# Sending row maxima and reciprocals to all lanes over memory, from the second batch on

## The reference

```
q = (layernorm(x) @ Wq + bq)            # 4 batches x 256 rows, 32 heads of 128
k, v = split(ctx @ Wkv + bkv)           # 4 batches x 1601 context rows, 8 kv heads of 128
scores = einsum("blkgd,bmkd->bkglm", q, k) / sqrt(128)
attn = softmax(scores, axis=-1)
o = einsum("bkglm,bmkd->blkgd", attn, v)
x = x + tanh(g_xattn) * (o @ Wo + bo)
x = x + tanh(g_ffn) * ffn(layernorm(x)) # base matrix, top 2 of 8 LoRA experts
```

## Time and profile before

| | |
|---|---|
| time, median of 3 runs | 2336.55 us (2336.43 to 2344.85) |
| the profiled execution's own time | 2337.85 us |
| its span, first to last instruction | 2335.9 us |
| busy: PE, DVE, ACT, POOL | 98%, 78%, 72%, 70% |
| mean granted TensorE clock | 0.996 |

### The profile page before, as it was taken

The page is one execution under the profiler, slowest core; times in us unless marked ns, Lnnn a source line. Parts: engine busy times, 40 slices in busy tenths (PEclk is TensorE's granted clock), DMA queues, the critical chain, the costliest instruction groups (busy, mean ns, idle before and its releaser), DMA issues.

```text
span 2335.9 us, 37750 instructions
## 1 busy us (share of the span) xinstructions
PE 2289.8 (98%) x12569; PEld 1956.9 (84%) x12569; DVE 1822.1 (78%) x3162; ACT 1685.2 (72%) x3208; POOL 1631.9 (70%) x1372
## 2 busy tenths in 40 slices
PE   7999999999999999999999999999999999999988
PEld 6888888888888888888888888888888888888864
DVE  5887888879778787877878778787878768778775
ACT  4776777767777776777767777776777767777763
POOL 5897987967667786866757867774865757656672
PEclk9999999999999999999999999999999999999999
DMA  7444334354133233335133243223423122122211
GB/s 256 147 147 142 117 129 144 133 201 144 59 124 114 93 122 100 98 108 185 59 104 105 77 133 115 102 92 115 143 82 109 66 79 82 46 100 73 82 37 54
DMA packets 122591, 258.11 MB, mean 111 GB/s; under 512 B 13344, under 2 KB 46624, under 8 KB 122144
## 3 DMA queue, kind: packets, MB, share of 16 engines
q1 hardware_dynamic: 122400, 255.71, 32.4%
HBM read 188.81 MB, written 66.86 MB: 109 GB/s over the span
## 4 chain that ended last, share of the span: by engine, by line
PE 87%; DVE 5%; POOL 4%; ACT 2%; issue 2%; DMA 0%; ACTq 0%; SPq 0%; POOLq 0%; DVEq 0%
PE psW L381 13%; PE psW L382 12%; PE psW L383 12%; PE psW L577 7%; PE psS L383 7%; PE psS L381 7%; PE psS L382 7%; PE psW L579 7%; PE psW L578 7%; PE psW L436 2%; PE psW L444 2%; POOL xs L766 2%; POOL pl L770 1%; DVE mrun L1194 1%; DVE psum_ L1221 1%
## 5 line engine op out<-in xcount | busy, mean ns | idle before, releaser
L766 POOL TENSOR_TENSOR xs<-xs,mb 128x512 f32<-128x512 f32 (+1 forms) x832 | 1069.2, 1314 | 518.1 <-ACT mb L837 518.1
L1194 DVE TENSOR_TENSOR mrun<-psS,mrun 128x512 f32<-128x512 f32 (+1 forms) x704 | 483.9, 687 | 380.3 <-ACT xs L837 377.7
L837 ACT ACTIVATE xs<-psS 128x512 f32<-128x512 f32 (+1 forms) x832 | 496.7, 597 | 212.2 <-PE psS L383 202.6
L930 ACT ACTIVATE ph<-xs 128x512 fp32r<-128x512 f32 (+1 forms) x832 | 520.6, 626 | 0.9 <-PE psW L579 0.9
L991 DVE TENSOR_TENSOR pl<-psP,ph 128x512 fp32r<-128x512 f32 (+1 forms) x672 | 459.5, 684 | 54.8 <-ACT ph L930 49.0
L1221 DVE TENSOR_TENSOR psum_<-psP,psum_ 128x512 f32<-128x512 f32 (+1 forms) x672 | 457.3, 681 | 0.0
L927 ACT ACTIVATE psP<-xs 128x512 f32<-128x512 f32 (+1 forms) x672 | 402.4, 599 | 3.0 <-POOL xs L766 1.5
L381 PE MATMUL psS<-ql,kh 128*128 128x512 f32 (+1 forms) x832 | 344.1, 414 | 1.1 <-DVE ql L1014 1.1
L577 PE MATMUL psW<-ph,vh 128*128 128x512 f32 (+1 forms) x832 | 336.6, 405 | 5.8 <-POOL pl L770 4.0
L383 PE MATMUL psS<-qh,kl 128*128 128x512 f32 (+1 forms) x832 | 328.1, 394 | 0.0
L382 PE MATMUL psS<-qh,kh 128*128 128x512 f32 (+1 forms) x832 | 328.1, 394 | 0.0
(11 more groups left out here) (185 smaller groups left out, 4562.5 us busy)
## 6 DMA issues: line engine op xcount, KB each, us to landing
wqh<-scr_wq SPq DMA_DIRECT2D x96, 256.0 KB, 2.6
wql<-scr_wq SPq DMA_DIRECT2D x96, 256.0 KB, 2.9
woh<-scr_wo SPq DMA_DIRECT2D x48, 512.0 KB, 3.3
wol<-scr_wo SPq DMA_DIRECT2D x48, 512.0 KB, 4.4
scr_wq<-wqh SPq DMA_DIRECT2D x32, 256.0 KB, 2.0
scr_wq<-wql SPq DMA_DIRECT2D x32, 256.0 KB, 2.5
scr_wo<-woh SPq DMA_DIRECT2D x16, 512.0 KB, 2.6
scr_wo<-wol SPq DMA_DIRECT2D x16, 512.0 KB, 4.0
```

Source lines behind the costliest of these rows:

```text
L766: eng.tensor_tensor(tile, tile, mb[0:rows_of(t), U % 2, :], ALU.subtract).then_inc(s_sub)
L837: return eng.activation(hi, src, ACT.Copy)
L930: eng.activation(ph[0:rows, T % RP, :], xs[0:rows, T % RX, :], ACT.Exp).then_inc(s_h)
L1194: eng.tensor_tensor(run, psS[0:rows, s % 2, :], a, ALU.max).then_inc(s_m)
```

## The change

For units 16 to 61 the maxima, and for units 16 to 60 the reciprocals, no longer pass through PE and ACT. SP writes the 128 x 4 values to a small tensor in memory (2 KB), waits for that, and reads it back with a broadcast over partitions, 512 values on each of 128 lanes (256 KB), straight into `mb` or `rbc`. The jobs `b` and `r` go for these units, and the other jobs are laid out anew in `AT_MEM`. DVE makes `nm` and `rinv` first in its slot, ahead of the running maximum. The multiplication by `rbc`, `oh`, `ol` and `o0` come one slot later. So that the values lie in memory in the right order, the transposes of `m` and `s` take every fourth column.

```diff
+    MEM_LO, MEM_MAX, MEM_SUM = 16, UN - 2, UN - 3
+    def max_by_mem(U):
+        return MEM_LO <= U < MEM_MAX
+    def sum_by_mem(U):
+        return MEM_LO <= U < MEM_SUM
+    def by_pe(U, by_mem):
+        return sum(not by_mem(u) for u in range(U + 1))
+    def on_slot(V):
+        return 9 if sum_by_mem(V) else 8
 ...
+    AT_MEM = [
+        "m q0 k3 - q1 s v0 v1 v2 v3 - o0 o1",
+        "m,v4 v5 q0 v6 k0 s,v7 q1 k1 v8 v9 v10 o0 o1",
+        "m,v11 k2 v12 q0 k3 s - - q1 - - o0,x0 o1,x1",
+        "m q0 - k0 q1 s k1 - - k2 - o0 o1",
+    ]
-                    UN + 1: "- - - - - s - r - - o0 o1"}.get(U, AT[U % 4])
+                    UN + 1: "- - - - - s - r - - o0 o1"}.get(U, (AT_MEM if U >= 2 and sum_by_mem(U - 2) else AT)[U % 4])
+                if kind == "b" and max_by_mem(n) or kind == "r" and sum_by_mem(n):
+                    continue
 ...  TensorE
+                    cols = src.rearrange("l (p k) -> l k p", k=4)[:, k, :] if every_fourth else src[:, k * 128:(k + 1) * 128]
+                    m = eng.transpose(o[:, k * 128:(k + 1) * 128], cols, ident[:, :])
-                if s % NT == 10 and s // NT >= 2:
+                if s // NT >= 2 and s % NT == on_slot(s // NT - 2) + 2:
                     emptied(("pv", s // NT - 2, 0), s_ol, s // NT - 1)
 ...  SyncE
+            def max_to_lanes(n):
+                i = n - MEM_LO
+                sp.wait_ge(s_nm, n + 1)
+                if i >= 2:
+                    sp.wait_ge(s_md, 16 * (i - 1))
+                eng.dma_start(scr_m[n % 2], nm[:, n % 2, :]).then_inc(s_mw, 16)
+                sp.wait_ge(s_mw, 16 * (i + 1))
+                if n >= 2:
+                    sp.wait_ge(s_sub, NT * (n - 1))
+                eng.dma_start(mb[:, n % 2, :], scr_m[n % 2].rearrange("p k -> (p k)").partition_broadcast(128)).then_inc(s_md, 16)
+            def sum_to_lanes(n):
+                # the same with s_r, rinv, scr_r, s_rw, s_on, rbc and s_rd
 ...
             for s in range(SLOTS):
+                if t == 1 and max_by_mem(U - 1):
+                    max_to_lanes(U - 1)
+                if t == 6 and sum_by_mem(U - 2):
+                    sum_to_lanes(U - 2)
 ...  GpSimd, in take_off
+                if max_by_mem(U):
+                    pool.wait_ge(s_md, 16 * (U - MEM_LO + 1))
+                else:
+                    pool.wait_ge(s_mb, by_pe(U, max_by_mem))
 ...  ScalarE
-                if s % NT == 8 and 0 <= V < UN:
+                if 0 <= V < UN and s % NT == on_slot(V):
                     act.wait_ge(s_on, V + 1)
 ...  VectorE
+            def goes_first(kind, n, part):
+                return kind == "m" and max_by_mem(n) or kind == "s" and sum_by_mem(n)
             for s in range(SLOTS):
+                for j in jobs.get(s - 1, []):
+                    if goes_first(*j):
+                        after_job(*j)
 ...
-                if t == 8 and 0 <= U - 2 < UN:
+                if 0 <= V < UN and t == on_slot(V):
                     dve.wait_ge(s_pv, NT * (V + 1))
+                    if sum_by_mem(V):
+                        dve.wait_ge(s_rd, 16 * (V - MEM_LO + 1))
+                    else:
+                        dve.wait_ge(s_rb, by_pe(V, sum_by_mem))
```

More of the change, by code:

```diff
@@ L19, in gated_block @@
 def gated_block(nc: bass.Bass, x, ctxT, gx, gf, wq, bq, wk, wv, bkv, wo, bo, bw, rw, la, lb,
-                scr_x, scr_b, scr_w, scr_c, out):
+                scr_x, scr_b, scr_w, scr_c, scr_m, scr_r, out):
     F32 = mybir.dt.float32
@@ L221, in gated_block @@
         s_out = sem("s_out")
+        s_mw = sem("s_mw")
+        s_md = sem("s_md")
+        s_rw = sem("s_rw")
+        s_rd = sem("s_rd")
         s_s = sem("s_s")
@@ L431, in proj_q, with turn @@
                 emptied(("q", U, h), s_ql, 2 * U + h + 1)
-            def turn(key, src, done, by, v):
+            def turn(key, src, done, by, v, every_fourth=False):
                 o = take(key)
                 for k in range(4):
-                    m = eng.transpose(o[:, k * 128:(k + 1) * 128], src[:, k * 128:(k + 1) * 128], ident[:, :])
+                    cols = src.rearrange("l (p k) -> l k p", k=4)[:, k, :] if every_fourth else src[:, k * 128:(k + 1) * 128]
+                    m = eng.transpose(o[:, k * 128:(k + 1) * 128], cols, ident[:, :])
                 m.then_inc(done)
@@ L505, in job @@
                     pe.wait_ge(s_m, 12 * (n + 1))
-                    turn(("m", n, 0), mrun[:, n % 2, :], s_mt, s_nm, n + 1)
+                    turn(("m", n, 0), mrun[:, n % 2, :], s_mt, s_nm, n + 1, max_by_mem(n))
                 elif kind == "s":
@@ L513, in job @@
                         pe.wait_ge(s_ap, 2 * (n - NU + 1))
-                    turn(("s", n, 0), psum_[:, n % 2, :], s_su, s_r, n + 1)
+                    turn(("s", n, 0), psum_[:, n % 2, :], s_su, s_r, n + 1, sum_by_mem(n))
                 elif kind == "b":
                     pe.wait_ge(s_nm, n + 1)
-                    spread(("b", n, 0), nm[:, n % 2, :], s_bt, s_mb, n + 1)
+                    spread(("b", n, 0), nm[:, n % 2, :], s_bt, s_mb, by_pe(n, max_by_mem))
                 elif kind == "r":
                     pe.wait_ge(s_r, n + 1)
-                    spread(("r", n, 0), rinv[:, n % 2, :], s_rt, s_rb, n + 1)
+                    spread(("r", n, 0), rinv[:, n % 2, :], s_rt, s_rb, by_pe(n, sum_by_mem))
                 elif kind == "x":
@@ L648, in load_ctx @@
                 eng.dma_start(f32(cl[:, :, lo:lo + w]), scr_c[b - 1, 1, :, :, lo:lo + w]).then_inc(s_lc[c], 16)
+            def max_to_lanes(n):
[9 more added lines that the diff above has]
+            def sum_to_lanes(n):
+                i = n - MEM_LO
+                sp.wait_ge(s_r, n + 1)
+                if i >= 2:
+                    sp.wait_ge(s_rd, 16 * (i - 1))
+                eng.dma_start(scr_r[n % 2], rinv[:, n % 2, :]).then_inc(s_rw, 16)
+                sp.wait_ge(s_rw, 16 * (i + 1))
+                if n:
+                    sp.wait_ge(s_on, n)
+                eng.dma_start(rbc[:, :], scr_r[n % 2].rearrange("p k -> (p k)").partition_broadcast(128)).then_inc(s_rd, 16)
             eng.dma_start(x_raw, x[:, 0:2, :]).then_inc(s_in["x"], 16)
@@ L762, in take_off @@
                 U, t = divmod(T, NT)
-                pool.wait_ge(s_mb, U + 1)
+                if max_by_mem(U):
+                    pool.wait_ge(s_md, 16 * (U - MEM_LO + 1))
+                else:
+                    pool.wait_ge(s_mb, by_pe(U, max_by_mem))
                 pool.wait_ge(s_e, T + 1)
@@ L940, in _ @@
                     elif kind == "b":
-                        act.wait_ge(s_bt, n + 1)
+                        act.wait_ge(s_bt, by_pe(n, max_by_mem))
                         if n >= 2:
@@ L945, in _ @@
                     elif kind == "r":
-                        act.wait_ge(s_rt, n + 1)
+                        act.wait_ge(s_rt, by_pe(n, sum_by_mem))
                         if n:
@@ L1128, in row_max @@
                 if n >= 2:
-                    dve.wait_ge(s_bt, n - 1)
+                    dve.wait_ge(s_bt, by_pe(n - 2, max_by_mem))
+                    if max_by_mem(n - 2):
+                        dve.wait_ge(s_mw, 16 * (n - 2 - MEM_LO + 1))
                 eng.tensor_reduce(nm[:, n % 2, :], bank_of(("m", n, 0)).rearrange("p (j k) -> p j k", j=4),
@@ L1148, in after_job @@
                     if n >= 2:
-                        dve.wait_ge(s_rt, n - 1)
+                        dve.wait_ge(s_rt, by_pe(n - 2, sum_by_mem))
+                        if sum_by_mem(n - 2):
+                            dve.wait_ge(s_rw, 16 * (n - 2 - MEM_LO + 1))
                     settle(eng.tensor_reduce(ssum[:, n % 2, :], bank_of(("s", n, 0)).rearrange("p (j k) -> p j k", j=4),
@@ L1194, in _ @@
                         eng.tensor_tensor(run, psS[0:rows, s % 2, :], a, ALU.max).then_inc(s_m)
-                if t == 8 and 0 <= U - 2 < UN:
-                    V = U - 2
+                V = U - 2
+                if 0 <= V < UN and t == on_slot(V):
                     dve.wait_ge(s_pv, NT * (V + 1))
-                    dve.wait_ge(s_rb, V + 1)
+                    if sum_by_mem(V):
+                        dve.wait_ge(s_rd, 16 * (V - MEM_LO + 1))
+                    else:
+                        dve.wait_ge(s_rb, by_pe(V, sum_by_mem))
                     eng.tensor_tensor(bank_of(("pv", V, 0)), bank_of(("pv", V, 0)), rbc[:, :], ALU.mult).then_inc(s_on)
-                if t == 9 and 0 <= U - 2 < UN:
-                    V = U - 2
+                if 0 <= V < UN and t == on_slot(V) + 1:
                     dve.wait_ge(s_oh, V + 1)
@@ L1205, in _ @@
                 for j in jobs.get(s - 1, []):
-                    if j[0] not in "ms" or not TN - NT < s <= TN:
+                    if (j[0] not in "ms" or not TN - NT < s <= TN) and not goes_first(*j):
                         after_job(*j)
@@ L1228, in _ @@
                     for j in jobs[s]:
-                        if j[0] in "ms":
+                        if j[0] in "ms" and not goes_first(*j):
```

(1 more changed line is left out.)

## The result

| | before | after |
|---|---|---|
| median of 4 runs each | 2339.14 us (2336.43 to 2344.85) | 2421.65 us (2419.82 to 2428.47) |
| span of the profiled execution | 2335.9 us | 2419.2 us |
| mean granted TensorE clock | 0.996 | 0.985 |

The changed kernel takes 1.0355 times as long (95% interval 1.0325 to 1.0385), 82.5 us more. The forecast was 2351, its range ended at 2376.

A forecast was written before the change was run, and what follows sets the result against it. PE, busy 98%, was taken to bound the kernel. Losses of 56.2 us less gains of 42.2 gave net +14 on 2337.85, so 2351.9, and 1.3 lower for the median: 2351 (likeliest 2342 to 2362, range 2324 to 2376).

The forecast's parts named there:

- 40.0 for 91 spreads: On PE, removing 46 spreads of maxima and 45 of reciprocals at 0.44 us each saves 40.0 us.
- losses that it laid to the bare slots: PE waits behind bare slots: 1.1 and 0.35 us (U%4=0), 1.1 and 1.5 (U%4=2), 0.5 (U%4=3) a unit.
- That it broadcasts costs nothing: In the read back from memory, sending one row to all lanes adds no time, judged from the `bo` broadcast's 6.2 us.
- the read at 2.6: The 256 KB read into `mb` or `rbc` lands in 2.6 us, within a round trip of 4.65 us.
- Rival (c): Round trip takes 6.0 us or more, as short-row writes are dearer: 2371 us, at 7.5 us 2417; chance 0.14.
- one of the write: Sign that the prediction is wrong: the small write to memory takes 3 us or more.
- The rule for `mb`: M starts after `mb` arrives (9.1 us into the unit) plus 2.56 for S0 and S1, unless the DVE sum is later.
- the queue, 4.0 + 7.4: On SP's queue, context tiles delay `mb` in 4 units (4.0 us); context loads delay `rbc` in units 30 and 46 (7.4).
- (a): Slots shrink and nothing is late, engines catching up: 2294 us with all waits hidden, 2329 with half; chance 0.17.
- (b): Losses just cancel the gain: no queue terms and a trip of 3.6 us give 2333 us; chance 0.25.
- (d): Removed spreads only filled time in which PE would wait anyway, so none of the 40 is gained: 2390 us; chance 0.03.
- A transpose worth its whole row: On PE, 364 transposes at 0.276 us each would save 100 us instead of 40, giving 2291 us; chance 0.01.

The follow-up runs named there:

- e3: Changed kernel without any DMA for maxima and reciprocals, stale values used, new job lists and later output chain kept: 2339.87 us, ratio 1.0015 to the unchanged kernel.
- e10: Changed kernel with filler matmuls ahead of PE's waits in slots 5 and 6 of units with U%4=0 and 3: 2411.09 us, ratio 1.032 to the unchanged kernel.
- e1: Changed kernel with both broadcast reads replaced by 256 KB reads of 128 different rows of `x`, writes and waits kept: 2383.74 us.
- e5: Changed kernel with the context load's last chunk issued behind the sum's round trip, not ahead, in units 30 and 46: 2409.74 us, ratio 1.0307 to the unchanged kernel.
- e9: Changed kernel with memory only for maxima in units U%4=1,2 and reciprocals in U%4=0,1,3, some jobs moved: 2325.4 us, again 2322.37; ratios 0.9947, 0.9945 to unchanged.

## Why the prediction was wrong

**Right: what is gained, and what the layout costs.** Nothing in the runs contradicts 40.0 for 91 spreads: a slot with `b` alone lasts 1.75 before, an empty one 1.39 in e3, and the next slot is shorter by 0.08. The losses that it laid to the bare slots are there without any trip, in e3: 1.4 in slot 6 and 0.4 in slot 11 of kind 0 (forecast 1.1 and 0.35), 1.1 in slot 8 and 1.6 in slot 11 of kind 2 (1.1 and 1.5), 0.6 in slot 11 of kind 3 (0.5). Gains of 42.2 against layout losses of 38.2 (44.8 less the 6.6 that hang on the trip) give 2333; e3 measured 2339.9. The 7 us between lie mostly in kinds 0 and 2, where e3's units are some 0.35 longer than forecast.

**Wrong: "That it broadcasts costs nothing", and the read at 2.6.** This is the step that failed first. The argument from the earlier trace rows was bad: a transfer that lands 0.2 later than the one ahead of it on a full queue doesn't show what it costs alone. The read took 4.4 and 4.0, and the whole trip 6.28 in unit 52. Rival (c), "the trip is 6.0 or more", had the length right and the reason wrong: it named the short rows of the write, and the write took 1.7 and 1.4. The Trainium skill ("DMA: Bandwidth & Descriptors", Specifications) has transfers under 512 bytes do a read-modify-write; a 2 KB write that lands sooner than the 2.0 of 256 KB shows no large surcharge for it, and whether it holds a small one no run here shows. The prediction named no time of the read at which it would be wrong, only one of the write.

**The rule for `mb` was right.** With 6.28 in place of 4.65, M stands at 10.72 + 2.56 = 13.3 in kinds 0 and 3 (measured 13.25). By the prediction's own rule kind 3 then loses 1.6 more and kind 0 0.7 more a unit: 18 + 8, hence 2377. Quiet units measured the same: an excess of 3.0 in kind 3 against 0.8 in e3, of which 0.6 was forecast, and 2.5 in kind 0 against 1.8.

**Missing altogether: the clock.** The prediction priced each wait at its own length and left PE's clock at full speed, without a word. Eleven stretches at half clock lie in units 16 to 61, with 47.7 us of PE's work in them: 23.8 of the 82 us. e10 shows that the loss follows from PE standing idle. From which wait on it falls, the runs don't say: unit 55 kept its clock with waits of 0.55 and 1.13, and unit 36 with 1.83 and 1.13; unit 35 lost it for 3.4 us with 0.58 and 1.14, unit 20 for 6.8 with 3.1 in all. In units 20, 35 and 40 the fall even begins within a wait.

**Too small: the queue, 4.0 + 7.4.** Its mechanism was right, and the clock has to be taken out before its size can be judged. Units 30 and 46 are 5.6 and 6.4 longer than in e3, and the work at half clock in them costs 1.9 and 3.1; what is left, 3.7 and 3.3, is the forecast's 3.7 each. Kept tiles were forecast to delay `mb` in four units of kind 3, a us each. Those (23, 27, 39 and 43) lost 0.3 to 0.9 each beyond a quiet unit, less their clock; the extra of units 35 and 51 is the clock alone. But kinds 0 and 2 lost too, where nothing was forecast: units 20, 24, 28, 36 and 40 14.8, of which 9.2 are the clock, units 22, 26, 38 and 42 7, others some 3. And in unit 62, which the prediction overlooked, the last units' loads stand ahead of the write: 4.6, some work at half clock included. Without the clock of units 16 to 61 the queue comes to some 29 us in place of 11.4.

**The sum.** 2377, 18 more for the queue and 24 for the clock give 2419. The 7 us of layout above come on top, and the parts outside units 18 to 62 are 4 shorter than in e3: 2422, against 2421.65. The split is worked out from the starts of the slots and is an estimate, since work at half clock can lie inside a wait. That the trip, the order in the queue and the clock each cost time is shown by e1, e5 and e10.

**The rivals.** (a), that engines catch up and nothing is late, falls with e3: without any trip PE still waits, and the time is 2339.9 and not 2294 to 2329. (b) needed a trip of 3.6 and a write that passes the loads, and had neither. Had (d) been right, that the spreads only filled time, e3 would have come 40 above 2333; it came 7 above. A transpose worth its whole row is ruled out by the slots of 1.75 and 1.39. What stays open: why a fresh and a repeated row are slower to read, and why the surcharge for the repeated row is seen on `mb` and hardly on `rbc`. Moving the kept context tiles off SP's queue was not tried.

## What to carry to other kernels

Before work leaves the bound engine for a longer path, list by stage how late the value may come, and move it only where that slack is longer than the path, as e9 did for 13 us where the whole change lost 82. Price a path that the trace does not show from a row of its own kind: a full queue hides what a transfer costs alone. And a wait of the matmul engine is not paid at its length only: where two waits of PE, of 1.7 to 3.2 us together, stood close to each other here, the work behind them could run at half clock.

## What the runs showed of the hardware

- 2 KB of 16-byte rows, written to memory on a quiet queue, landed after 1.4 us, sooner than 256 KB (2.0). Behind two context loads of 898 KB each, still under way, it took 7.7 and landed 0.2 after the second: it did not pass them.
- 256 KB read from memory, medians to landing in us: 2.6 for weights before the change, 3.0 and 3.2 for 128 rows of `x` in the places of `rbc` and `mb`, 3.1 and 3.9 for one row repeated 128 times, 4.0 and 4.4 if that row has just been written.
- In unit 39 a wait of PE of 2.05 us was followed by 6.8 us at a granted clock of 0.50. With seven matmuls more (0.234 us each) ahead of the two matmuls that wait there, idle times of 1.70 and 0.59 were left and the clock stayed at 1.00.
